# When the modulation of an adaLN block is computed: two components first, four later in column tiles

## The reference

```python
mod = (_silu(L0_c) @ L0_wmod).reshape(L0_c.shape[0], 6, 1, -1)
sa, ca, ga, sb, cb, gb = (mod[:, 0], mod[:, 1], ..., mod[:, 5])
ga = (2 * (ga >= 0) - 1) * jnp.maximum(jnp.abs(ga), 0.25)      # gb likewise
h = _layernorm(x) * (1 + ca) + sa
x = x + ga * attention(h)     # layernorm, K, V, Q, sum over rows of cos-similar K*V, output product
h = _layernorm(x) * (1 + cb) + sb
x = x + gb * ffn(h)           # up, relu, down, plus an expert product
```

## Time and profile before

| | us |
|---|---|
| median of 3 runs | 386.73 (384.7 to 387.5) |
| the profiled execution, whole | 386.43 |
| its span, first to last instruction | 384.6 |
| PE busy | 367.0 |
| DVE busy | 255.4 |
| ACT busy | 166.7 |
| POOL busy | 113.3 |

### The profile page before, as it was taken

The page is one execution under the profiler, slowest core; times in us unless marked ns, Lnnn a source line. Parts: engine busy times, 40 slices in busy tenths (PEclk is TensorE's granted clock), DMA queues, the critical chain, the costliest instruction groups (busy, mean ns, idle before and its releaser), DMA issues.

```text
span 384.6 us, 4649 instructions
## 1 busy us (share of the span) xinstructions
PE 367.0 (95%) x1664; PEld 286.9 (75%) x1664; DVE 255.4 (66%) x515; ACT 166.7 (43%) x293; POOL 113.3 (29%) x110
## 2 busy tenths in 40 slices
PE   4997999899997999989999999999999999999996
PEld 0155888678885888868788878888788878887885
DVE  0677799869978488876887559727550855084354
ACT  1337388884427821075314681247114612541210
POOL 0114683276932528425163151910000001000000
PEclk9988899999999899999999999999999999999999
DMA  7995964050030000000000002100200110011002
GB/s 222 378 388 191 348 258 168 0 164 2 2 82 2 0 0 2 27 2 2 0 27 2 0 0 111 28 2 27 82 2 0 55 56 0 0 57 55 2 0 109
DMA packets 10951, 27.42 MB, mean 71 GB/s; under 512 B 1185, under 2 KB 1569, under 8 KB 9777
## 3 DMA queue, kind: packets, MB, share of 16 engines
q1 hardware_dynamic: 10928, 27.13, 19.8%
HBM read 22.90 MB, written 4.23 MB: 71 GB/s over the span
## 4 chain that ended last, share of the span: by engine, by line
PE 66%; DVE 12%; issue 7%; ACT 6%; DMA 4%; POOL 2%; SPq 1%; DVEq 0%; ACTq 0%; POOLq 0%
PE ps L1032 19%; PE ps L1034 19%; PE ps L1033 19%; PE ps L1039 3%; PE ps L1056 2%; DMA xs<-in_wmod 2%; DMA xs<-in_X 2%; ACT sqj L444 2%; DVE hb L657 1%; PE ps L1047 1%; ACT ps L493 1%; DVE ps L690 1%; PE ps L1159 1%; PE ps L1160 1%; ACT t_hi L495 1%
## 5 line engine op out<-in xcount | busy, mean ns | idle before, releaser
L1032 PE MATMUL ps<-w_hi,t_hi 128*128 128x512 f32 x192 | 75.7, 394 | 0.0
L1034 PE MATMUL ps<-w_hi,t_lo 128*128 128x512 f32 x192 | 75.2, 392 | 0.0
L1033 PE MATMUL ps<-w_lo,t_hi 128*128 128x512 f32 x192 | 75.2, 392 | 0.0
L1032 PE MATMUL ps<-t_hi,w_hi 128*128 128x512 f32 x128 | 51.6, 403 | 0.0
L1032 PE MATMUL ps<-w_hi,g_hi 128*128 128x512 f32 (+1 forms) x132 | 51.3, 389 | 0.3 <-DVE g_lo L743 0.3
L1034 PE MATMUL ps<-w_hi,g_lo 128*128 128x512 f32 (+1 forms) x132 | 50.6, 383 | 0.0
L1033 PE MATMUL ps<-w_lo,g_hi 128*128 128x512 f32 (+1 forms) x132 | 50.5, 383 | 0.0
L1034 PE MATMUL ps<-t_hi,w_lo 128*128 128x512 f32 x128 | 50.4, 393 | 0.0
L1033 PE MATMUL ps<-t_lo,w_hi 128*128 128x512 f32 x128 | 50.4, 393 | 0.0
L683 DVE TENSOR_TENSOR t_lo<-ps,t_hi 128x512 fp32r<-128x512 f32 x32 | 21.8, 688 | 32.9 <-ACT t_hi L495 32.6
L1032 PEld LDWEIGHTS ps<-w_hi,t_hi 128*128 128x128 f32 x192 | 36.5, 190 | 7.6
(11 more groups left out here) (130 smaller groups left out, 613.8 us busy)
## 6 DMA issues: line engine op xcount, KB each, us to landing
xs<-in_X SPq DMA_DIRECT2D x4, 1024.0 KB, 7.5
stage<-in_w SPq DMA_DIRECT2D x4, 1024.0 KB, 6.8
out<-xs SPq DMA_DIRECT2D x15, 256.0 KB, 2.0
xs<-in_wmod SPq DMA_DIRECT2D x3, 1024.0 KB, 9.8
xs<-in_wmod SPq DMA_DIRECT2D x8, 256.0 KB, 7.0
stage<-in_w SPq DMA_DIRECT2D x8, 256.0 KB, 9.6
gate_bc<-mod_rows SPq DMA_DIRECT2D x8, 256.0 KB, 6.7
gate_bc<-in_wmod SPq DMA_DIRECT2D x1, 1024.0 KB, 11.9
```

What stands on the lines that cost most here:

```text
L1032: mm(dst, l_hi, r_hi, start=start, stop=False)
L1033: mm(dst, l_hi, r_lo, start=False, stop=False)
L1034: return mm(dst, l_lo, r_hi, start=False, stop=stop)
```

## The change

Six modulation components are no longer all computed at the start. Only `ca` and `sa` are. The other four are computed together by `mod_rest`, on PE behind K/V tile 1 of batch 0, each on its own 32 columns of the array (`tile_position=(0, 32*j)`) into one bank; ACT takes the result out twice, DVE makes the gate rows (`mod_gates`), PE turns the block (`mod_turn`) behind K/V tile 2, and DVE takes `cb` and `sb` as columns out of it (`mod_cols`). Batch 0's rows are scaled straight from x, and go tile by tile through normalisation, transposes and splitting (`h_row0`, `transposes0`, `t0_evac`, `t0_split`). K/V weight pieces are split in another division of labour. Banks are renumbered. The SP queue is reordered.

```diff
@@ SP queue, behind the loads of ca, x of batch 0 (now two halves), sa, ident, K/V pieces @@
-            sp.dma_start(x_slot(1), wmod[2]).then_inc(wm_in[2], 16)
-            sp.dma_start(gate_bc[:], wmod[4]).then_inc(wm_in[4], 16)
...
             load_x(1)
+            sp.wait_ge(mod_ps, 2)
+            sp.dma_start(MODS[0][1], wmod[MODS[0][0]]).then_inc(wm_in[MODS[0][0]], 16)
             sp.wait_ge(row_out, 32)
             load_modulation(1)
+            sp.dma_start(MODS[1][1], wmod[MODS[1][0]]).then_inc(wm_in[MODS[1][0]], 16)
+            sp.dma_start(w_raw[2], w[2]).then_inc(w_in[2], 16)
+            sp.wait_ge(wlo_k, NC)
+            sp.dma_start(MODS[2][1], wmod[MODS[2][0]]).then_inc(wm_in[MODS[2][0]], 16)
+            sp.wait_ge(wlo_v, NC)
+            sp.dma_start(MODS[3][1], wmod[MODS[3][0]]).then_inc(wm_in[MODS[3][0]], 16)
+            sp.dma_start(bo_bc[:], brow[0:1, 2 * D:3 * D].to_broadcast([P, D])).then_inc(const_in, 16)
+            sp.wait_ge(mod_ps, 3)
+            sp.dma_start(w_raw[3], w[3]).then_inc(w_in[3], 16)
+            sp.wait_ge(gate_s, 1)
+            sp.dma_start(mod_rows[ROW_GA], gate_rows[0:B, :]).then_inc(gate_out, 16)
+            sp.dma_start(mod_rows[ROW_GB], gate_rows[32:32 + B, :]).then_inc(gate_out, 16)
             sp.wait_ge(gate_out, 32)
             for b in range(B):
                 sp.dma_start(gate_bc[:, b * D:(b + 1) * D],
                              mod_rows[ROW_GA, b:b + 1, :].to_broadcast([P, D])).then_inc(ga_in, 16)
-            sp.wait_ge(wlo_k, NC)
-            sp.dma_start(w_raw[3], w[3]).then_inc(w_in[3], 16)
             sp.wait_ge(wlo_q, NC)
             load_x(2)
-            sp.wait_ge(mod_ps, 6)
+            sp.wait_ge(modt_ps, 1)
             load_x(3)
@@ POOL: rstd_x(1) also waits for h1_s; start @@
+            low_kv(0, 0)
+            low_kv(1, 0)
+            rstd_h(0, 0, 1)
...
             low_part(2, whi, (1,) * NC, wlo_q)
@@ ACT, attention(0), behind norm_sums(0, 1) @@
+                    act.wait_ge(mod_ps, 3)
+                    nc.scalar.activation(mod_abs, ps[:, MOD_BANK, :], ACT.Abs, scale=2.0).then_inc(abs_s, 1)
+                    act.wait_ge(abs_s, 1)
+                    nc.scalar.activation(mod_raw, ps[:, MOD_BANK, :], ACT.Copy).then_inc(mod_row_s, 1)
                     split_hi(3)
                     x_sums(2)
@@ ACT, start @@
+            for k in range(3):
+                split_hi_kv(0, k)
+                split_hi_kv(1, k)
+            normalise(0, 0, 1)
+            t0_evac(0)
+            normalise(0, 1, 1)
+            split_hi_kv(0, 3)
+            split_hi_kv(1, 3)
+            normalise(0, 2, 1)
+            t0_evac(1)
+            normalise(0, 3, 1)
             split_hi(2)
+            t0_evac(2)
+            t0_evac(3)
@@ DVE, attention(0) @@
                 if b == 0:
                     x_shift(1)
+                    t0_split(2)
                 kv_products(b, 0)
+                if b == 0:
+                    t0_split(3)
@@ DVE, behind kv_products(0, 1) @@
                 elif b == 0:
+                    mod_gates()
                     h_row(1, 0)
@@ DVE, behind kv_products(0, 2) @@
                     h_shift(1, 2, 2)
+                    mod_cols()
@@ PE @@
+            def mod_rest():
+                for _, s in zip(range(4), MODS):
+                    pe.wait_ge(wm_in[s[0]], 16)
+                for k in range(NC):
+                    for j in range(4):
+                        last = mm(ps[32 * j:32 * j + 32, MOD_BANK, :], sc[:, k * B:k * B + 32],
+                                  MODS[j][1][:, k * D:(k + 1) * D], start=(k == 0), stop=(k == NC - 1),
+                                  tile_position=(0, 32 * j))
+                last.then_inc(mod_ps, 1)
...
+                else:
+                    transposes0(2)
+                    transposes0(3)
                 for t in range(1, NT):
+                    if b == 0 and t == 1:
+                        pe.wait_ge(h1_s, NT)
                     kv_tile(b, t)
+                    if b == 0 and t == 1:
+                        mod_rest()
+                    if b == 0 and t == 2:
+                        mod_turn()
                 for c in range(NC):
                     if b == 0 and c == 0:
                         pe.wait_ge(wlo_q, NC)
+                        pe.wait_ge(sign_s, 1)
+                    if b == 0 and c == 1:
+                        pe.wait_ge(col_sb, 2)
```

More of the change, by code:

```diff
@@ L83, in build @@
         rows = v_sb[0:B]
[L84 to L86 removed]
+        mod_raw, mod_abs, mod_sign, gate_rows = (xs[:, ((B - 1) * NT + i) * D:((B - 1) * NT + i + 1) * D] for i in range(4))
         col = sb("col", [P, COLS])
@@ L133, in build @@
         x_in = sem("x_in")
+        x0_in = [sem(f"x0_in{i}") for i in range(2)]
         wm_in = [sem(f"wm_in{i}") for i in range(NCOMP)]
@@ L148, in build @@
         mod_sb = sem("mod_sb")
+        mod_row_s = sem("mod_row_s")
+        sign_s, gate_s = sem("sign_s"), sem("gate_s")
+        modt_ps, col_sb = sem("modt_ps"), sem("col_sb")
+        t0_full = sem("t0_full")
         whi_k, whi_v = sem("whi_k"), sem("whi_v")
@@ L318, in rstd_x @@
                 pool.wait_ge(xve_s, g + 1)
+                if g == 1:
+                    pool.wait_ge(h1_s, NT)
                 power(xrs[:], xve[:], NT, xrs_s)
@@ L559, in _ @@
                                  ACT.Copy).then_inc(wg_hi_s, 1)
[L560 to L567, removed]
+            act.wait_ge(mod_ps, 2)
+            nc.scalar.activation(rows[:, 1, :], ps[0:B, 1, :], ACT.Copy).then_inc(mod_sb, 1)
+            for k in range(3):
[9 more added lines that the diff above has]
+            normalise(0, 3, 1)
             split_hi(2)
-            act.wait_ge(mod_sb, 6)
+            t0_evac(2)
+            t0_evac(3)
             for b in range(B):
@@ L649, in h_row @@
                 h = h_row_of(g, t)
[L650 to L657, removed]
+                dve.wait_ge(scaled_s, n + 1 - NT)
+                if t == 0:
+                    dve.wait_ge(ca_in, g * 32)
+                v.tensor_tensor(h, h, sa_bc[:], ALU.add).then_inc(h1_s, 1)
             def h_stats(g, t):
@@ L911, in _ @@
[L911 to L919, removed]
-            for c in range(2, NC):
-                split_v(c)
-                t_split(0, c)
+            for t in range(NT):
+                if t % 2 == 0:
+                    dve.wait_ge(x0_in[t // 2], 16)
+                v.bn_stats(xst[:, t, :], xs[:, tok(0, t)]).then_inc(xst_s, 1)
@@ new lines, in _, with h_row0 @@
+            x_aggr(0)
+            dve.wait_ge(bc_ps, 1)
+            for t in range(NT):
+                v.scalar_tensor_tensor(h_row_of(0, t), xs[:, tok(0, t)], xmv[:, t, 0:1], ps[:, 2, :],
+                                       ALU.subtract, ALU.mult).then_inc(scaled0_s, 1)
+            def h_row0(t):
+                if t == 0:
+                    dve.wait_ge(xrs_s, 1)
+                    dve.wait_ge(bc_ps, 2)
+                dve.wait_ge(scaled0_s, t + 1)
+                h = h_row_of(0, t)
+                v.scalar_tensor_tensor(h, h, xrs[:, t:t + 1], ps[:, 3, :], ALU.mult, ALU.add).then_inc(h1_s, 1)
+                h_stats(0, t)
@@ new lines, in split_lo_kv, with mod_gates @@
+            def split_lo_kv(i, k):
+                dve.wait_ge(whi_v if i else whi_k, k + 1)
+                dve.wait_ge(wlo_v if i else wlo_k, k)
+                v.tensor_tensor(w_lo[:, W_ORDER[i], k, :], w_raw[i][:, k * D:(k + 1) * D],
+                                w_hi[:, W_ORDER[i], k, :].bitcast(f32), ALU.subtract).then_inc(wlo_v if i else wlo_k, 1)
+            def mod_gates():
+                dve.wait_ge(mod_row_s, 1)
+                v.tensor_scalar(mod_sign, ps[:, MOD_BANK, :], 0.0, 0.5, ALU.is_ge, ALU.subtract).then_inc(sign_s, 1)
+                dve.wait_ge(sign_s, 1)
+                v.scalar_tensor_tensor(gate_rows, mod_abs, 2 * MIN_GATE, mod_sign, ALU.max, ALU.mult).then_inc(gate_s, 1)
@@ new lines, in mod_cols @@
+            def mod_cols():
+                dve.wait_ge(modt_ps, 1)
+                turned = ps[:, MODT_BANK, :].rearrange("p (c j b) -> p j b c", c=NC, j=4)
+                v.tensor_scalar(cb_col[:].rearrange("p (b c) -> p b c", c=NC), turned[:, 2, 0:B, :], 1.0, None,
+                                ALU.add).then_inc(col_sb, 1)
+                v.tensor_copy(sb_col[:].rearrange("p (b c) -> p b c", c=NC), turned[:, 3, 0:B, :]).then_inc(col_sb, 1)
+            h_row0(0)
+            h_aggr(0, 0, 1)
@@ L923, in _ @@
+            h_row0(1)
+            h_aggr(0, 1, 1)
+            h_shift(0, 0, 1)
+            h_row0(2)
+            h_aggr(0, 2, 1)
+            h_shift(0, 1, 1)
+            h_row0(3)
+            h_aggr(0, 3, 1)
+            h_shift(0, 2, 1)
+            t0_split(0)
+            h_shift(0, 3, 1)
+            split_lo_kv(0, 3)
+            split_lo_kv(1, 3)
+            t0_split(1)
             for b in range(B):
```

169 lines of the change are left out of this document (76 added, 93 removed).

## The result

| | before | after |
|---|---|---|
| median of 4 runs, us | 387.12 (384.7 to 388.0) | 399.36 (397.95 to 401.57) |
| profiled execution, us | 386.43 | 401.57 |
| its span, us | 384.6 | 399.8 |
| PE busy, us | 367.0 | 357.4 |

The account below looks back on a forecast made before the run. PE sets the end only where DVE and ACT deliver; `x_mean(2)` at 66.8 plus 7.1, 0.45 and slowed Q chunk 1 puts batch 1's transposes at 78.5, 9.7 us later. Less 0.6: 386.4 + 9.1 = 395.5 us, range 389.5 to 402.5.

Parts of the forecast that it names:

- `mod_rest`: PE behind K/V tile 1: sixteen matmuls with neighbours only partly beside each other, 7.3 us; said not to matter below about 7.
- The mechanism: Late wQ, then late gates, delay batch 2's x; DVE idles at `x_mean(2)`, PE over 10 us ahead of Q chunk 1.
- the gain of the start: Less work ahead of K/V tile 0 lets it start near 28.3 us instead of 38.8, 10.5 us earlier.
- the load of wQ: SP queue: issued at 27.0 us behind `h1_s`, 2.6 MB at 373 GB/s, 7 us, landing at 34.0.
- DVE's stretch from `x_shift(1)` to the end of `kv_products(0, 1)`: Batch 0's attention: 7.3 us as before plus two splits of 0.65, from 42.1 to 50.7 us.
- the load of batch 2's x: SP queue, behind the gates' trip: 6.9 us behind other traffic, or 5.5; 6.9 taken.
- The gates' trip through DRAM: SP queue behind `gate_s`: two issues 0.6 us, write landing 2.0, four broadcasts 1.98, all ahead of batch 2's x.
- the clock: PE at Q chunk 1 after its pause: first six matmuls slow, 0.45 in place of 0.23, costing 1.4 us.
- (b): Shorter chain: wQ lands 3.5 us earlier, `mod_rest` takes 3.6, the gates' trip and load are shorter; 389.5 us, chance 0.12.
- (c): No wait in `x_mean(2)`, which runs before about 57 us, so PE keeps its clock; 383.4 us, chance 0.04.
- Rival (a): Column tiles do not run beside each other: `mod_rest` ends at 56.0, all behind 6.7 us later; 402.2 us, chance 0.14.
- Rival (d): The start does not come early, the tile-by-tile chain of ACT, POOL and DVE being worse; 397 to 400 us, chance 0.08.

Follow-up runs that it names:

- e1_x2_early: Changed kernel with the load of batch 2's x ahead of the wait for the gates in the SP queue: 386.85 us, 1.003 of the kernel before.
- e6_wq_early: Changed kernel with only wQ's load moved ahead of batch 1's x; batch 2's x still late: 392.52 us, 1.017 of the kernel before.
- e8_x2_mid: Changed kernel with batch 2's x loaded between the gate rows' writes and the wait for their landing: 394.27 us, 1.021 of the kernel before.
- e2_cols_early: Changed kernel with `mod_cols` ahead of `x_mean(2)` on DVE, batch 2's x still loaded late: 397.59 us, 1.031 of the kernel before.
- e3_tiles_seq: Changed kernel with the 16 column-tile matmuls issued component by component, four in a row on the same 32 columns: 398.11 us.
- e4_x2_cols: Changed kernel with batch 2's x loaded ahead of the gates and `mod_cols` ahead of `x_mean(2)`: 384.30 us, 0.995 of the kernel before.

## Why the prediction was right, and where its sizes were off

The forecast was 395.5 us in a range of 389.5 to 402.5; the median is 399.36. The narrower range of the forecast itself, 392 to 398.5, did not hold. Point by point, the measured side read from the profiled execution (401.57 us):

| step | forecast, us | measured, us |
|---|---|---|
| K/V tile 0 starts | 28.3 | 27.91 |
| wQ issued, landed | 27.0, 34.0 | 26.10, 37.1 |
| `x_shift(1)` | 42.1 | 45.10 |
| `mod_rest` | 7.3 | 3.6 |
| Q chunk 0 ends | 63.6 | 63.7 |
| `gate_s` | 52.3 | 56.8 |
| gate rows landed after the last issue | 2.0 | 1.15 |
| x of batch 2, issue to use | 6.9 | 8.6 |
| `x_mean(2)` | 66.8 | 72.03 |
| from there to `col_sb` | 7.55 | 7.4 |
| PE's wait ahead of Q chunk 1 | 10.7 | 15.8 |
| Q chunk 1 | 4.1 | 5.2 |
| batch 1's first transposes | 78.5 | 84.70 |

**The mechanism** held at every joint: the gain of the start is real, DVE waits for wQ, the gates come late, batch 2's x is queued behind them, DVE stops in `x_mean(2)`, PE stops ahead of Q chunk 1 with a fallen clock, and only 0.8 us is won back later (forecast 0.6). e1_x2_early, e6_wq_early and e8_x2_mid each shorten one link, and `x_mean(2)` and the end move with it: `x_mean(2)` comes 13.2, 8.1 and 7.6 us earlier between the traces, and the medians fall by 12.5, 6.8 and 5.1 us. The traces give more because the changed kernel's is of its longest run.

**The first mis-sized term** is the load of wQ: 11.0 us from issue to use instead of 7.0, so it was there at 37.1 instead of 34.0. The forecast counted 2.6 MB at 373 GB/s from the moment of the `h1_s` wait. The table by stretch (the last two numbers are DMA share and GB/s) shows a queue without rest from 25.0 us on:

```profile
17.00:25.00 8.00, 2.21 (x6) 1.01 (x6) 6.54 (x17) 4.78 (x11) 7.03 (x8) 0.67 0.74 264
25.00:37.10 12.10, 9.95 (x44) 8.39 (x45) 8.14 (x20) 6.46 (x14) 2.59 (x3) 0.79 0.99 405
```

From 25.0 to 37.1 us 4.9 MB were moved (12.1 x 405), 2.3 MB more than counted. An estimate from these rows splits them. Of the 3.1 MB issued from 17.8 to 19.7 (`bkv_bc`, `rot_sb`, batch 1's x, component 2) only 2.1 MB (8.0 x 264) had moved at 25.0, so 1.0 MB still lay ahead. The other 1.2 MB or so belong to what was issued behind wQ, at 28.4 to 30.0: two more components of 1 MB each and `bo_bc`. The forecast left out both.

**The second** is DVE's stretch from `x_shift(1)` to the end of `kv_products(0, 1)`: 9.7 us instead of 8.6. It was taken from before, where POOL was quiet during the three small operations of `kv_products(0, 0)`; now POOL multiplies batch 1's rows beside them, and from the first of them to the next operation 3.6 us pass instead of 1.1. The `kv_sum` behind them gives back 1.0 us and a wait that is gone 0.3 us. With 3.0 us from wQ and 0.4 us more for the gates, `gate_s` is 4.5 us late.

**The third** is the load of batch 2's x, 8.6 instead of 6.9. In e2_cols_early and e3_tiles_seq, whose queues are the same, it was 7.2 and 7.4, so most of this miss is the spread between executions. e8_x2_mid shows the price of the four broadcasts ahead of it: with them behind, the load took 5.0. The gates' trip through DRAM went the other way: from `gate_s` to the issue of the load 3.6 us passed instead of 4.6. The write of the gate rows had landed, by the wait behind it, 1.15 us after its last issue; the prediction took 2.0, which is also the figure that it quotes from the Trainium skill (DMA: Bandwidth & Descriptors, the table of two cost components), and here the measurement decides.

**The fourth** is the clock. The forecast let six matmuls run at the lower level, as at 38.7 to 41.5; nearly all of Q chunk 1 did. The table by stretch of the changed kernel has the granted clock as third number from the end:

```profile
63.60:79.50 15.90, 0.11 (x2) 0.01 (x1) 7.33 (x22) 9.04 (x23) 1.54 (x3) 0.62 0.56 197
79.50:84.70 5.20, 5.20 (x12) 4.02 (x13) 3.98 (x9) 2.74 (x6) 1.13 (x2) 0.51 0.00 0
84.70:88.30 3.60, 3.60 (x21) 3.08 (x20) 0.97 (x2) 2.59 (x4) 0.00 (x0) 1.00 0.02 5
```

Twelve matmuls at 0.51 (the level of 1.2 GHz) take 5.2 us, those of the next chunk, at full clock, 2.8. The pause costs 15.8 us and 2.4 more behind it. In e3_tiles_seq, behind a pause of 12.9 us, the same chunk took 4.2 us, what the forecast said, so this size too differs between executions.

The terms close: 4.5 us at `gate_s`, less 1.0 to the issue, plus 1.7 for the load make `x_mean(2)` 5.2 us late; with 1.1 us of clock, less 0.1, the transposes are 6.2 us late, and 0.2 more won back leaves 6.0 of the 6.1 us between 395.5 and 401.57.

**`mod_rest`** was over-priced, 7.3 against 3.6 us, and the text was right that this would not matter: the gates waited for DVE. That Q chunk 0 ended when forecast is luck: PE had two waits that the forecast put at nothing, 1.1 us for the bank of K/V tile 2 and 2.2 us for ACT ahead of `mod_turn`, and they took up nearly all that `mod_rest` had saved. The 4.7 us that the prediction draws from the Trainium skill (TensorE: Matmul & The Clock Gate, Part 3) is not what the figure named there gives: 14 us divided by 2.38 is 5.9, an estimate, and the 3.6 us measured are less than either.

**Smaller slips of the prediction.** Two of the seven waits for `t_lo`, 2.2 of the 6.2 us, lie ahead of K/V tile 0 (at 34.87 and 38.04), not behind it. Half of (b) and the rest of (c) make a chance of 0.07, not 0.08.

**The rivals.** Rival (a) is refuted for the order in which the kernel issues its tiles. Rival (b) did not come about, since wQ landed later, not earlier, though `mod_rest` and the write of the gates were as short as it assumed. Rival (c) needed `x_mean(2)` before 57 us; with the order of e1_x2_early, which makes DVE's stall vanish, it came at 58.9, and the time was that of the kernel before; without the wait for the bank as well, in e4_x2_cols, it was 384.30, near the 383.4 that (c) names. Rival (d) did not occur; the start came even 0.4 us earlier than summed.

Not settled: how much of wQ's late landing is due to the transfers still under way ahead of it and how much to those issued behind it; no run took one away and left the other. In e8_x2_mid 1 MB of broadcasts, issued 1.0 us behind a load of 1 MB, left that load at 5.0 us, so transfers behind a load need not delay it.

## What to carry to other kernels

An earlier start of the engine that sets the end is worth only what the second engine's queue can follow, so find the next instruction of each other engine that waits and ask what it hangs on. When a value is made later, look at every transfer that stands behind its store in the same queue: here a load that needed nothing of the gates cost 12 us by standing behind them. The semaphore that the profile names at the stalled engine is the last link; follow it back until a chain begins, before the bank or buffer it guards is changed.

## What the runs showed of the hardware that was not expected

**Column tiles.** Sixteen float32 matmuls of 512 columns on four tiles of 32 columns took 3.6 us (42.18 to 45.82), as long as four of them on the whole array in the earlier trace rows: full concurrency. The second record of the first tile starts at 42.60, behind the first records of the other three (42.18, 42.18, 42.19), although it precedes them in program order. In e3_tiles_seq whole matmuls change places: the second tile's first starts at 43.38, ahead of the first tile's fourth (its seventh record, 44.23). The Trainium skill (TensorE: Matmul & The Clock Gate, Part 3) states the concurrency, and the trace agrees; it also says that matmuls start in program order, and here the trace does not agree. Issued component by component, the same matmuls took 8.8 us.

**DVE beside POOL.** While POOL multiplied 128x512 operands in SBUF (46.24 to 50.13 us), three small DVE operations took 0.90, 1.39 and 1.40 us; a tile later, with nothing on POOL but operands of one or two columns, the same three took 0.28, 0.28 and 0.43:

```profile
46.77 0.90 DVE L751 TENSOR_TENSOR prod<-cross 128x128 f32<-128x128 f32 x1
47.59 1.39 DVE L754 TENSOR_TENSOR prod<-prod 128x128 f32<-128x128 f32 x1
49.02 1.40 DVE L756 TENSOR_TENSOR prod<-prod,rot_sb 128x256 f32<-128x256 f32 x1
...
53.98 0.28 DVE L751 TENSOR_TENSOR prod<-cross 128x128 f32<-128x128 f32 x1
54.18 0.28 DVE L754 TENSOR_TENSOR prod<-prod 128x128 f32<-128x128 f32 x1
54.50 0.43 DVE L756 TENSOR_TENSOR prod<-prod,rot_sb 128x256 f32<-128x256 f32 x1
```
```profile
46.24 3.89 POOL L382 TENSOR_TENSOR hb<-z,ca_bc 128x512 f32<-128x512 f32 x3 [0.25 <-ACT z L507]
```

In e6_wq_early, where DVE is earlier and POOL's multiplications start only with the third of them, the same three of the first tile are short as well:

```profile
41.62 0.28 DVE L751 TENSOR_TENSOR prod<-cross 128x128 f32<-128x128 f32 x1
41.81 0.28 DVE L754 TENSOR_TENSOR prod<-prod 128x128 f32<-128x128 f32 x1
42.13 0.46 DVE L756 TENSOR_TENSOR prod<-prod,rot_sb 128x256 f32<-128x256 f32 x1
```
```profile
42.27 4.28 POOL L382 TENSOR_TENSOR hb<-z,ca_bc 128x512 f32<-128x512 f32 x3
```

In the kernel before, POOL's multiplications (50.96 to 55.07) fell on `kv_sum` (L718, at 51.11), which took 1.56 us; in the changed kernel it took 0.60 (at 50.94, POOL idle). DVE's product that reads PSUM (L749, at 46.17) took 0.68 us beside POOL as ever. So POOL's work on SBUF lengthens DVE's operations that have all operands in SBUF; by what means, no run shows.

**A short pause is enough.** In e1_x2_early PE stood for only 3.3 us, and its clock was 0.62 on average over the next 4.5 us. Longer pauses did not cost steadily more: Q chunk 1 took 4.4 us behind 3.3 us of waiting, 5.2 behind 9.3 (e8_x2_mid), 4.7 behind 11.7 (e6_wq_early), 4.2 behind 12.9 (e3_tiles_seq) and 5.2 behind 15.8, against 2.8 at full clock. Behind the 0.5 us of e4_x2_cols the granted clock stayed at 1.00 (67.0 to 70.0 us).

```profile
66.30:70.80 4.50, 4.47 (x13) 3.48 (x14) 4.01 (x9) 2.78 (x6) 1.13 (x2) 0.62 0.67 279
```
